# Gather indices of the first attention: kept on chip for all groups, in place of a load for each group

## The reference, cut to what matters

```python
def _L0_gnn_ref(x, edge_attr, edge_index, Wq, bq, Wk, bk, We, be, Wv, bv):
    Qh = (x @ Wq.T + bq).reshape(n, H, D)          # H = 4 heads of D = 16
    Kh = (x @ Wk.T + bk).reshape(n, H, D)
    Vh = (x @ Wv.T + bv).reshape(n, H, D)
    Ee = (edge_attr @ We.T + be).reshape(-1, H, D)
    score = (Kh[src] * Qh[dst] * (1.0 / np.sqrt(D)) * Ee).sum(-1)
    score = jnp.exp(jnp.clip(score, -5.0, 5.0))
    msg = Vh[src] * score[..., None]
    wV = jax.ops.segment_sum(msg, dst, num_segments=n)
    return wV.reshape(n, H * D)

x = _layernorm(x + _L0_gnn_ref(x, edge_attr_64, edge_index, ...), axis=-1)
```

## Time and profile before

| | |
|---|---|
| timed runs, median of 3 (lowest to highest) | 1912.07 us (1908.1 to 1912.09) |
| span of the profiled execution | 2674.2 us |
| preparations in it | 0 to 47 us |
| first attention in it (98 groups, 784 gathers) | 47 to 1471 us |
| all that follows | 1471 to 2674 us |
| busy in the span | PE 1501.4 us (56%), PEld 1250.3 (47%), DVE 1423.4 (53%), ACT 1008.8 (38%), POOL 1227.4 (46%) |
| L634, the gathers, x784 | 763.2 us busy, 974 ns each; POOL idle before them 674.3 us, 459.3 of it till the load of `idx` |

### The profile page before, as it was taken

The page is one execution under the profiler, slowest core; times in us unless marked ns, Lnnn a source line. Parts: engine busy times, 40 slices in busy tenths (PEclk is TensorE's granted clock), DMA queues, the critical chain, the costliest instruction groups (busy, mean ns, idle before and its releaser), DMA issues. The chain is left out here.

```text
span 2674.2 us, 43621 instructions
## 1 busy us (share of the span) xinstructions
PE 1501.4 (56%) x12903; PEld 1250.3 (47%) x12903; DVE 1423.4 (53%) x3785; ACT 1008.8 (38%) x2221; POOL 1227.4 (46%) x1328
## 2 busy tenths in 40 slices
PE   3555555555555654555555774754134656555795
PEld 2444444434444443344434673753033645444785
DVE  6455555555555554555555787871023534434685
ACT  3333333333333333333333651750003534434683
POOL 2555555555555554545553460546724343444100
PEclk7677777777777767777777787885556777777897
DMA  5222222222222222222221210022201111111100
GB/s 116 54 58 56 58 59 57 59 57 61 57 58 60 56 59 52 60 55 58 59 57 35 62 59 3 2 87 34 35 17 33 37 34 37 32 41 33 40 26 14
DMA packets 125233, 128.69 MB, mean 48 GB/s; under 512 B 80959, under 2 KB 88435, under 8 KB 124840
## 3 DMA queue, kind: packets, MB, share of 16 engines
q0 software_dynamic: 35776, 62.74, 10.4%
q1 hardware_dynamic: 63778, 57.41, 7.8%
q10 hardware_dynamic: 25542, 6.81, 1.1%
HBM read 116.64 MB, written 10.20 MB: 47 GB/s over the span
## 5 line engine op out<-in xcount | busy, mean ns | idle before, releaser
L634 POOL DMA_INDIRECT shared<-kv_tab,idx x784 | 763.2, 974 | 674.3 <-DMA idx<-in_src 459.3
L836 PE MATMUL bank<-key_hot,lo_hot 128*128 128x350 f16 x784 | 220.8, 394 | 586.5 <-DVE count L698 392.4
L836 PEld LDWEIGHTS bank<-key_hot,lo_hot 128*128 128x128 f16 x784 | 59.3, 101 | 703.4 <-issue 690.4
L2282 POOL DMA_INDIRECT count<-att_tab,count x240 | 228.3, 951 | 301.7 <-PE bank L2827 193.4
L698 DVE TENSOR_TENSOR count<-count,bank 128x350 f32 x392 | 205.4, 524 | 109.4 <-issue 73.6
L735 DVE TENSOR_TENSOR acc<-acc,bank 65x64 f32 x98 | 21.3, 217 | 429.2 <-remote 425.8
L779 ACT ACTIVATE expo<-score 128x32 f32<-128x32 f32 x98 | 22.5, 229 | 587.3 <-DVE score L716 566.9
L769 ACT ACTIVATE lo_dist<-iota_neg,tile_lo 128x128 f16<-128x128 f32 x784 | 238.5, 389 | 0.0
L2656 ACT ACTIVATE shared<-shared 128x126 f32<-128x126 bf16 x336 | 144.4, 484 | 172.0 <-PE bank L2804 88.6
L683 DVE TENSOR_SCALAR key_hot<-iota_key,tile_key 128x350 f16<-128x350 f16 x784 | 193.3, 319 | 0.0
L851 PEld LDWEIGHTS bank<-hots,msg 128*65 128x65 f32 x1568 | 183.8, 221 | 0.4 <-DVE msg L725 0.4
(11 more groups left out here) (528 smaller groups left out, 3237.8 us busy)
## 6 DMA issues: line engine op xcount, KB each, us to landing
shared<-in_edge_attr SPq DMA_DIRECT2D x97, 256.0 KB
shared<-lo_tab SPq DMA_DIRECT2D x28, 512.0 KB
shared<-kv_tab,idx POOLq DMA_INDIRECT x784
count<-att_tab,count POOLq DMA_INDIRECT x240
qwin<-q_tab ACTq DMA_DIRECT2D x196, 16.0 KB
kv_tab<-count SPq DMA_DIRECT2D x1, 1600.0 KB, 10.4
idx<-in_src SPq DMA_DIRECT2D x97, 4.0 KB, 1.6
g_edge<-att_tab,count POOLq DMA_INDIRECT x94
```

The costliest lines, as they stand in the source:

```text
L634: nc.gpsimd.indirect_dma_start(kv[:, s, c, :], None, kv_tab, bass.IndirectOffsetOnAxis(ap=idx[:, s, c:c + 1], axis=0)).then_inc(kv_in[s], 16)
L836: last = nc.tensor.matmul(bank[6 + q % 2][:, 0:KC], lo_hot[:, c, :], key_hot[:, c, :], start=i == 0, stop=i == GT - 1)
L2282: nc.gpsimd.indirect_dma_start(ring[s][:, j, 0:D + 2], None, att_tab[1], bass.IndirectOffsetOnAxis(ap=src_i[:, t:t + 1], axis=0)).then_inc ...
```

## The change

The source nodes of all 98 groups are brought into SBUF once, in the preparations, as `idx_all` (it lies in `g_edge`), and so are the destinations. Both are loaded in rows, a group of 1024 edges on each of 98 partitions (`dst_g`, `src_g`: 4 KB a row), after DVE has filled the two tiles of 128x1024 (98 rows are used, and the last group isn't full). DVE converts both to floats (`dst_gf`, `src_gf`), PE turns them by eight transposes each (`turn_groups`: column c of a group's 128 partitions, for all groups), the destinations between the second and the third `multiply`, the sources between the sixth and the seventh, and DVE copies the results out of PSUM: the destinations to `dst_rel0` before the base is subtracted, the sources, as integers, to `idx_all` at its end. `dst_i` and its load and conversion go.

In the first attention SP loads no indices; the semaphores `idx_in` go. POOL waits for `slot_free` itself, ahead of the first gather of each group, and gathers by `idx_all[:, c, g:g + 1]`. The wait after the fifth gather goes. The later layers' loops are unchanged.

```diff
@@ -155,6 +155,9 @@
         g_edge = sb("g_edge", [P, RS, C, D + 4])
+        edge_words = g_edge[:, :, :, :].rearrange("p s c f -> p (s c f)")
+        idx_all = edge_words[:, 0:G * C].bitcast(i32).rearrange("p (c g) -> p c g", c=C)
+        src_g, src_gf = edge_words[:, 0:ST].bitcast(i32), edge_words[:, ST:2 * ST]
         hot = sb("hot", [P, C, W])
@@ -207,7 +210,7 @@
         holder[0] = starting
-        dst_i = sb("dst_i", [P, G, C], i32)
+        dst_g, dst_gf = sb("dst_g", [P, ST], i32), sb("dst_gf", [P, ST])
         lowest = sb("lowest", [P, 4 * P])
@@ -242,6 +246,10 @@
         by_pool, by_dve = free_at + 5000, free_at + 7500
+        def turned_groups(b):
+            return bank[b][:, 0:C // 2 * G].rearrange("p (c g) -> p c g", c=C // 2)
@@ -272,8 +280,9 @@
                 sp.dma_start(be_row[:, :], be.rearrange("(a n) -> a n", a=1).to_broadcast([BF, D])).then_inc(s_rest, 16)
-                sp.dma_start(dst_i[:, 0:G - 1, :], dst[0:full].rearrange("(g p c) -> p g c", p=P, c=C)).then_inc(s_edges, 16)
-                sp.dma_start(dst_i[0:PL, G - 1, :], dst[full:E].rearrange("(p c) -> p c", c=C)).then_inc(s_edges, 16)
+                for into, of in ((dst_g, dst), (src_g, src)):
+                    sp.dma_start(into[0:G - 1, :], of[0:full].rearrange("(g e) -> g e", e=ST)).then_inc(s_edges, 16)
+                    sp.dma_start(into[G - 1:G, 0:E - full], of[full:E].rearrange("(a e) -> a e", a=1)).then_inc(s_edges, 16)
                 sp.dma_start(attc[:, :], attn_w.rearrange("(k p) -> p k", p=D), allow_slow_non_contiguous=True).then_inc(s_rest, 16)
@@ -322,7 +331,8 @@
             def _(dve):
-                nc.vector.memset(dst_i[:, G - 1, :], int(NONE))
+                nc.vector.memset(dst_g[:, :], int(NONE))
+                nc.vector.memset(src_g[:, :], 0)
                 nc.vector.memset(dst_r[:, TB - 1, :], int(NONE))
@@ -366,8 +376,10 @@
                 dve.drain().then_inc(s_base, 1)
-                dve.wait_ge(s_edges, 32)
-                nc.vector.tensor_copy(dst_rel0[:, :, :], dst_i[:, :, :])
+                dve.wait_ge(s_edges, 64)
+                nc.vector.tensor_copy(dst_gf[0:G, :], dst_g[0:G, :])
+                nc.vector.tensor_copy(src_gf[0:G, :], src_g[0:G, :])
+                dve.drain().then_inc(s_dstg, 1)
                 dve.wait_ge(s_basec, 1)
@@ -376,6 +388,9 @@
                 nc.vector.tensor_copy(group_base[:, :], bank[1][:, :])
+                dve.wait_ge(s_dstt, 1)
+                for k in range(2):
+                    nc.vector.tensor_copy(dst_rel0[:, :, k * C // 2:(k + 1) * C // 2], turned_groups(2 + 5 * k).rearrange("p c g -> p g c"))
                 dve.drain()
@@ -411,6 +426,9 @@
                 nc.vector.tensor_scalar(tile_hiw[:, :, :], tile_hi[:, :, :], float(WC), 1.0, ALU.mult, ALU.add)
+                dve.wait_ge(s_srct, 1)
+                for k in range(2):
+                    nc.vector.tensor_copy(idx_all[:, k * C // 2:(k + 1) * C // 2, :], turned_groups(3 + k))
@@ -429,6 +447,13 @@
                     last.then_inc(s_done, 1)
+                def turn_groups(of, first, second, turned):
+                    for c in range(C):
+                        last = nc.tensor.transpose(bank[first if c < C // 2 else second][:, c % (C // 2) * G:(c % (C // 2) + 1) * G],
+                                                   of[0:G, :].rearrange("g (p c) -> g c p", c=C)[:, c, :], ident[0:G, 0:G])
+                    last.then_inc(turned, 1)
@@ -452,13 +477,20 @@
                 pe.wait_ge(s_flat, 1)
-                for k in range(4):
+                for k in range(2):
+                    multiply(k)
+                pe.wait_ge(s_dstg, 1)
+                turn_groups(dst_gf, 2, 7, s_dstt)
+                for k in range(2, 4):
                     multiply(k)
...
                 last.then_inc(s_brep, 1)
-                for k in range(4, len(MM0)):
+                for k in range(4, 6):
+                    multiply(k)
+                turn_groups(src_gf, 3, 4, s_srct)
+                for k in range(6, len(MM0)):
                     multiply(k)
@@ -607,7 +639,6 @@
                         pass_on(sp)
-                        load_idx(sp, g, s, last, idx_in[s])
                         if last:
@@ -621,21 +652,14 @@
                 with pool.Fori(0, nj) as j:
-                    def indices(g):
-                        s = g % RS
-                        pool.wait_ge(idx_in[s], j * (uses(s) * 16) + (g // RS + 1) * 16)
-                        pass_on(pool)
-                    indices(0)
                     for g in range(G):
                         s = g % RS
+                        pool.wait_ge(slot_free, j * G + (g + 1))
+                        pass_on(pool)
                         for c in range(C):
                             nc.gpsimd.indirect_dma_start(
-                                kv[:, s, c, :], None, kv_tab, bass.IndirectOffsetOnAxis(ap=idx[:, s, c:c + 1], axis=0)
+                                kv[:, s, c, :], None, kv_tab, bass.IndirectOffsetOnAxis(ap=idx_all[:, c, g:g + 1], axis=0)
                             ).then_inc(kv_in[s], 16)
-                            if c == C // 2 and g + 1 < G:
-                                indices(g + 1)
```

More of the change, by code:

```diff
@@ L228, in build @@
         s_stored = short_sem("tables_stored")
+        s_dstg, s_dstt, s_srct = short_sem("dst_groups_ready"), short_sem("dst_groups_turned"), short_sem("src_groups_turned")
         early_sems = [s_zero, s_graph, s_gtail, s_x, s_xtail, s_w, s_const, s_edges, s_rest, s_rows, s_tiles, s_flat, s_wt, s_wcopied, s_base, s_basec,
-                      s_bdiag, s_brep, s_sp, s_spt, s_turned, s_copied, s_done, s_taken, s_ones, s_stored]
+                      s_bdiag, s_brep, s_sp, s_spt, s_turned, s_copied, s_done, s_taken, s_ones, s_stored, s_dstg, s_dstt, s_srct]
         kept = sem("kept")
@@ L585, in build @@
         begun = short_sem("a_begun")
-        slot_free, idx_in = short_sem("a_slot_free"), [short_sem(f"a_idx{s}") for s in range(RS)]
+        slot_free = short_sem("a_slot_free")
         ea_in, kv_in = [short_sem(f"a_ea{s}") for s in range(RS)], [short_sem(f"a_kv{s}") for s in range(RS)]
@@ L592, in build @@
         count_clear = short_sem("a_count_cleared")
-        loop_sems = [begun, slot_free, *idx_in, *ea_in, hot_ok, ea_t, ea_ts, hot_t, hot_ts, ee_ok, qd_ok, sc_ok, ex_ok, msg_ok, sum_ok,
+        loop_sems = [begun, slot_free, *ea_in, hot_ok, ea_t, ea_ts, hot_t, hot_ts, ee_ok, qd_ok, sc_ok, ex_ok, msg_ok, sum_ok,
                      cleared, q_in, key_ok, lo_ok, count_ok, bank_free, count_clear]
```

## The result

| | kernel before | kernel after |
|---|---|---|
| timed, median (lowest to highest) | 1912.02 us (1908.1 to 1923.3) | 1930.24 us (1926.8 to 1932.86) |
| ratio to before, 95% interval | 1 | 1.0083 (1.0062 to 1.0105) |
| span of the profiled execution | 2674.2 us; of a second one, 1915.2 us | 1925.0 us |

The account below looks back on a forecast made before the run. POOL's gathers, 10.0 us a group, were taken to bound the timed first attention. Preparations 4.6 us later (1.4 + 3.3 - 0.1) less 3.25 for the earlier start gave +1.35, so 1912.07 becomes 1913.4 us; range 1906 to 1918.5.

Parts of the forecast that it names:

- Loads: Preparations: 32-byte dst load goes, two loads of 4 KB rows come, nothing on the path waits; 0 to -0.3, taken -0.1 us.
- The fork: First attention, without profiler: POOL's eight gathers at 1.25 us, 10.0 a group, against the engines' chain at 9.0; POOL bound.
- Rivals 1, 3 and 4: 1: POOL isn't bound, +4.6 us, chance 0.31; 3: fewer small loads speed loop, 1904, 0.12; 4: relay bound, 1708, 0.03.
- rival 4: First attention: the relay (index load between slot and gather) stops POOL every group; removing it gives 1708 us; chance 0.03.
- Steady loop: First attention: index load and its wait go, a slot wait comes, the same 784 gathers remain; worth 0.
- Start: First attention: POOL's first gather comes 3.25 us sooner against the barrier, bounds 2.0 to 3.8; counts whole if POOL-bound.
- Rival 5: First attention: POOL still begins late without the relay, +4.6 us even if POOL-bound; chance held in that of rival 1.
- Memsets: Preparations, VectorE's front: two 128x1024 memsets of 0.91 us each lie on the path; 0.8 to 1.75, taken 1.4 us.
- Turns: Preparations, TensorE: two turns of eight transposes at 1.67 us each delay the kv_tab store by 3.3 us, bounds 1.5 to 3.6.
- rival 2: Preparations grow by only 2 us, pauses absorbing memsets and turns, while the earlier start counts; 1911 us, chance 0.11.
- The store near 39.4: Sign in the trace after: the store of kv_tab is issued near 39.4 us instead of 34.81.
- VectorE came to wait for gathers: Sign that the prediction is wrong: in the first attention VectorE waits for gathered rows.

Follow-up runs that it names:

- late_pool: split96 with POOL's first gather held back until ScalarE has cleared its counts; median 1916.29 us, ratio to before 1.0040.
- seven: split96 without the gathers of the eighth column of each group (98 of 784); median 1841.63 us, ratio to before 0.9632.
- prep_only: The changed kernel's preparations with the first attention's loop of before (index loads by SyncE for each group); median 1932.19 us, ratio to before 1.0120.
- split96: The changed kernel with each load of 97 rows cut into 96 and 1; median 1908.06 us, ratio to before 0.9983.
- direct: The kernel before with source indices loaded once in 32-byte pieces and the changed loop, no turns or large memsets; median 1906.34 us, ratio to before 0.9977.
- split89: The changed kernel with each load of 97 rows cut into 89 and 8; median 1925.5 us, ratio to before 1.0082.

## Why the prediction was wrong, point by point

**Loads: the step that failed.** "The load of dst in pieces of 32 bytes goes, and two loads in rows of 4 KB come. Nothing on the path waits for them now: 0 to -0.3, I take -0.1." In fact they cost 19.5 us: 17.1 of waiting at L380 and 2.4 of slower TensorE after it. I took large rows for cheap by their size alone and looked for nobody who waits, since nobody waits *now*; but the same change puts the turn of the destinations, and with it everything behind it on TensorE, after these loads. Before has loads of a prime number of rows too, but small ones (the last 53 rows of x, 13.2 KB in all), and no row of its trace gives the time of one, so the trace couldn't price it. The step should have had a wide bound and a rival of its own: a load whose row count doesn't divide over the DMA engines, at the rate of one. The rule stood in the page of the Trainium skill named above, and I had missed it.

**Which engine is the bound: right.** The fork was POOL with 8 x 1.25 = 10.0 us against a chain of 9.0. POOL it is, with 10.26 (0.978 + 0.305 a gather) against 9.4. late_pool shows that its start counts whole, seven that it yields first when relieved. Rivals 1, 3 and 4 fall by this: with POOL at work without a pause, neither late signals nor small loads nor the relay set the period. (The section of the Trainium skill that rival 4 names is about DMAs issued from GpSimd, and the relay's load is SyncE's; the figure that holds for it is the trace's 1.6 us.)

**Steady loop, 0: right** within what was measured. The periods of groups 10 to 90 are 10.22 (second profile of before), 10.21 (prep_only), 10.18 (after), 10.22 (split96 and direct). From the first gather to the last sum the kernels with the relay take 1010.0 and 1011.1 us and those without, all eight gathers in them, 1011.4 to 1013.2. That would be 1 or 2 us against the change, in one profile of each. POOL's idle time between gathers is the same, 238.6 us, in after and in the second profile of before; its gathers are busy for 766.5 us against 764.7 and 763.7 (prep_only). What stretches them stays open.

**Start, -3.25: right.** Store to first gather: 16.94 and 17.00 us in the two profiles of before, 13.79 after, 13.78 in split96, 13.73 in direct. That is 3.2, and it is worth its full length, as forecast for a bound POOL. Rival 5, a POOL that begins late anyway, is out.

**Memsets, 1.4: 2.1 at VectorE, 1.0 at ScalarE.** The first conversion comes at 12.17 in split96 and in the kernel after, at 10.06 in the first profile of before. The two are 0.91 each as computed, and on VectorE no pause absorbed any of it; the upper bound of 1.75 was 0.3 too low there. But ScalarE's first copy is 0.96 later only: in split96 the 21 transposes start 1.89 later (15.51 against 13.62) and take 3.75 us in place of 4.68. The same 21 take 4.74 in split89, and there the first copy is 1.95 later (26.68), so what the memsets cost at the store differs from execution to execution. Why the transposes differ isn't shown: the granted clock reads 1.00 over them in every profile. The rows of before:

```profile
10.06 0.61 DVE L349 TENSOR_SCALAR acc<-acc 128x896 int32<-128x896 int32 x1
...
24.73 0.39 ACT L315 ACTIVATE count<-bank 128x256 f32<-128x256 f32 x1 [1.67 <-PE bank L430]
...
26.74 1.06 PE L459 MATMUL bank<-lowest_diag,ones 128*128 128x128 f32 x8
```

and those of split96:

```profile
15.51 3.75 PE L467 MATMUL bank<-ident,count 128*128 128x128 f32 x21 [0.30 <-DVEq L368]
...
25.69 0.38 ACT L325 ACTIVATE count<-bank 128x256 f32<-128x256 f32 x1 [2.09 <-PE bank L449]
```

**Turns, 3.3: 1.3.** Without the wait, each of the two turns shows as a pair of ScalarE's copies 1.54 us after the pair before (26.34 to 27.88, and 30.72 to 32.26) where 0.91 is the distance without one: 0.63 each. Two things in the term were too large. A transpose costs 0.13 us here (L455, a turn of eight takes 1.02) and not the 0.223 of L441; and of the 1.02 us of a turn only 0.63 reaches ScalarE, the rest lies in time in which TensorE waits anyhow. L459, from which the term was read, takes 1.06 us in before (the row above) and costs the same 0.63 (26.94 to 28.48, less 0.91): it was already as long as a turn, and the 4 x 0.223 put on top of it were too much. The row of split96:

```profile
26.14 1.02 PE L455 MATMUL bank<-ident,dst_gf 98*128 98x98 f32 x8
```

Taken together split96's store is issued 37.03 - 34.81 = 2.2 us later, where 4.6 were forecast. Less the start's 3.2 that makes -1.0 us, or 0.9995 of before, inside split96's interval of 0.9965 to 1.0000. The 2.2 are the 0.96 of the memsets and the 1.26 of the turns, so of the terms of the sum these two were off by -0.4 and -2.0 us, and the loads by +19.6. With the loads cut, the kernel is what rival 2 described, preparations that grow by 2 us and a start that counts.

**The sum again.** With measured terms: first gather later by 19.5 (loads) + 2.2 (memsets and turns) - 3.2 (start) = 18.5 us; the rows say 70.36 - 51.75 = 18.6, and the timed ratio 1.0083 is 15.9 (11.9 to 20.1). Against the second profile of before the first gather is 12.0 later, since there the preparations ran at the lower clock. Which of the two the timed runs of before resemble isn't seen directly; that direct was 4.4 us faster and not 9.9 speaks for the first.

**What the text said would show it.** The two memsets (0.91 each), the first gather soon after the barrier, and an unchanged period were seen. The turns take 1.57 us (at the lower clock) and 1.03 in after, not 1.7. The store near 39.4 came at 56.57. "POOL's waits about as long a group as now (4 us)" and "14.5 us a group as before" weren't: both leaned on the shape of the 2674 us execution, in which TensorE's signals were late. The text had taken its time apart from the timed one and was right to; to then forecast its waits for the next profile was no use. "VectorE came to wait for gathers" was named as a sign of error and was none: it does so in the second profile of before too, 55 times.

## What to carry to other kernels

A load that is "off the path" must be priced with the waits that the same change puts behind it, and by the number of rows it is shared out by as well as their size: pad or cut it to a multiple of 16 rows (96 + 1 in place of 97 gave back 1% here). Ask of a profile first whether its span is that of the timed runs; if it isn't, take a second one before any wait in it is believed. When an engine issues without a pause, what it begins sooner or later counts in full.

## What the runs showed of the hardware

- Two DMAs of 97 rows of 4 KB took 34.1 us, 23.3 GB/s, with the DMA engines active for 0.08 of 16; cut as 96 and 1, all DMA traffic of that stretch, at 114 GB/s, was over by 15 us. SyncE's queue was held for 15.06 us by the issue of the second, and the loads of weights queued behind it began at 27.84.
- The granted clock of TensorE in the preparations isn't the same in each execution: from 24 to 38 us it was 0.93 in the first profile of before and 0.54 in the second, in which the same projections take 6.5 us longer.
- One profiled execution lasted 1.40 times the timed runs, the next of the same kernel 1.00 times. What was different in the first stays open.
